# Two transformer-like layers on one NeuronCore: the value products of attention uncut, and for two key tiles in one visit; constant activation biases

## What is computed

```python
x = _layernorm(x + _L0_attn_ref(x, ...))              # RWKV time mix and channel mix
x = _layernorm(x + _L0_xattn_ref(x, ctx_1024, mask))  # cross attention, 16 heads of 16, masked
x = _layernorm(x + _L0_ffn_ref(x, ...))               # SwiGLU with int weights
x = _layernorm(x + _L1_attn_ref(x, ...))              # RMS norm, RG-LRU, gated MLP
x = _layernorm(x + _L1_xattn_ref(ctx_1024, x, ...))   # queries: x, keys: context, 16 heads of 16
x = _layernorm(x + _L1_ffn_ref(x, ...))               # 8 experts, top 2
```

## Time and profile before

| | |
|---|---|
| median of 3 runs | 2336.97 us (2332.34 to 2337.36) |
| the profiled execution, its own time | 2334.47 us |
| its span | 2332.6 us |
| TensorE busy | 1915.1 us (82%), 9728 instructions |
| VectorE busy | 1112.3 us (48%) |
| ScalarE busy | 967.2 us (41%) |
| GpSimd busy | 221.6 us (9%) |
| value products L1056 | 4352 instructions of 256 columns, 349.1 us busy |
| score products L1080 | 1088, 370.9 us busy |
| first-pass products L1014 | 1280, 356.3 us busy |
| score exponentials L1162 | 1088, 593.8 us busy, idle before them 332.7 us |
| maxima L1207 | 512, 496.6 us busy, idle before them 129.0 us |

### The profile page before, as it was taken

The page is one execution under the profiler, slowest core; times in us unless marked ns, Lnnn a source line. Parts: engine busy times, 40 slices in busy tenths (PEclk is TensorE's granted clock), DMA queues, the critical chain, the costliest instruction groups (busy, mean ns, idle before and its releaser), DMA issues.

```text
span 2332.6 us, 31610 instructions
## 1 busy us (share of the span) xinstructions
PE 1915.1 (82%) x9728; PEld 819.8 (35%) x9729; DVE 1112.3 (48%) x1498; ACT 967.2 (41%) x1638; POOL 221.6 (9%) x188
## 2 busy tenths in 40 slices
PE   5789869999798757727999999999999539999980
PEld 2334323333343222312333333333332326666650
DVE  3652358774212415418877777767760401121115
ACT  2422317667211443310477677667677102222220
POOL 2030100000200103200000000000000240000005
PEclk8889979999899888965999999999999669999995
DMA  7000051011000000092000000000000720000003
GB/s 270 0 0 0 9 124 28 23 27 58 1 0 0 4 0 30 9 133 76 1 15 9 10 13 8 10 14 9 8 2 1 320 72 27 27 27 27 27 25 108
DMA packets 63288, 90.59 MB, mean 39 GB/s; under 512 B 14144, under 2 KB 56320, under 8 KB 61514
## 3 DMA queue, kind: packets, MB, share of 16 engines
q1 hardware_dynamic: 60106, 80.77, 12.0%
q0 software_dynamic: 3072, 8.39, 1.1%
HBM read 61.53 MB, written 27.20 MB: 38 GB/s over the span
## 4 chain that ended last, share of the span: by engine, by line
PE 55%; DVE 6%; issue 4%; POOL 3%; ACT 2%; DMA 2%; SPq 1%; DVEq 0%; ACTq 0%; POOLq 0%
PE ps L1056 9%; PE ps L1014 8%; PE ps L1699 8%; PE ps L512 8%; PE ps L1080 8%; PE ps L1714 5%; DVE arena L1207 2%; PE ps L1357 2%; DMA qparts<-arena 1%; POOL rows_in L1808 1%; PE ps L1115 1%; POOL arena L1813 1%; PE ps L440 1%; PE ps L1707 1%; ACT arena L1767 1%
## 5 line engine op out<-in xcount | busy, mean ns | idle before, releaser
L1162 ACT ACTIVATE arena<-ps 128x512 f32<-128x512 f32 x1088 | 593.8, 598 | 332.7 <-PE ps L1080 331.9
L1207 DVE TENSOR_REDUCE arena<-ps 128x1 f32<-128x802 f32 (+1 forms) x512 | 496.6, 990 | 129.0 <-PE ps L1014 119.9
L512 PE MATMUL ps<-arena 128*128 x832 | 380.6, 618 | 83.9 <-DVE arena L1498 24.5
L1014 PE MATMUL ps<-arena 97*128 97x401 bf16 (+2 forms) x1280 | 356.3, 362 | 80.0 <-DMA arena<-qparts 62.2
L1080 PE MATMUL ps<-arena 100*128 100x512 bf16 x1088 | 370.9, 383 | 9.2 <-issue 8.5
L1056 PE MATMUL ps<-arena 128*32 128x256 f32 x4352 | 349.1, 393 | 0.7 <-ACT arena L1162 0.3
L512 PEld LDWEIGHTS ps<-arena 128*128 128x128 f32 x832 | 163.1, 198 | 299.5 <-issue 299.5
L1699 PE MATMUL ps<-arena 128*128 x608 | 199.1, 470 | 29.2 <-ACT arena L1767 28.4
L1014 PEld LDWEIGHTS ps<-arena 97*128 97x128 bf16 x1280 | 94.7, 99 | 293.8 <-issue 167.2
L1894 DVE TENSOR_TENSOR arena<-ps,arena 128x352 f32<-128x352 f32 x76 | 39.9, 525 | 273.0 <-ACT arena L1774 273.0
L1204 DVE TENSOR_REDUCE arena<-ps 128x2 f32<-128x1024 f32 x128 | 154.3, 1220 | 25.6 <-PE ps L1014 25.6
(11 more groups left out here) (183 smaller groups left out, 1409.9 us busy)
## 6 DMA issues: line engine op xcount, KB each, us to landing
arena<-in_experts_w SPq DMA_DIRECT2D x8, 2176.0 KB, 17.7
arena<-qparts SPq DMA_DIRECT2D x192, 64.0 KB, 2.3
qparts<-arena SPq DMA_DIRECT2D x24, 256.0 KB, 6.0
rows_in<-arena SPq DMA_DIRECT2D x1, 5120.0 KB, 32.7
arena<-kparts SPq DMA_DIRECT2D x12, 416.0 KB, 23.9
arena<-rows_in SPq DMA_DIRECT2D x38, 128.0 KB
rows_out<-arena SPq DMA_DIRECT2D x38, 128.0 KB, 1.7
arena<-in_w_rwkv SPq DMA_DIRECT2D x1, 2560.0 KB, 12.5
```

Source lines behind the costliest of these rows:

```text
L512: ins = eng.matmul(out, w[:, k, m * P:(m + 1) * P], x[:, k, tok(c)], start=k == 0, stop=k == ktiles - 1)
L1014: ins = eng.matmul(slot_banks(s_static)[:, x, 0:n_keys], Qst[0:97, ring, heads[x], q * P:(q + 1) * P], Kst[0:97, ring * HG + heads[x], at: ...
L1162: eng.activation(probs[:, keys_of(u, kt) % 2, h, :], ring_bank(r), ACT.Exp, bias=0.0).then_inc(ring_read.sem, 1)
L1207: eng.tensor_reduce(MX[:, par, heads[0] * QT + q, n % 2:n % 2 + 1], got, AX.XY, ALU.max).then_inc(slot_free.sem, 1)
```

## The change

The value products are no longer cut: one product of 512 queries for each head and tile. In the second attention (not in the window) they are sent out for two tiles in one visit, at tiles 2, 4, 6, 8 and 10, behind score 2; tile 0 of the next unit sends out the last three. `probs` gets two more buffers there (`more_probs`, in the field `WB`, whose weights are no longer needed). The copy of bank 4 stays behind the fourth exponential of tile 0. The five bias columns, their memsets and the wait for them go; every activation gets its constant as a number. The fields of `arena` behind them move by 20 bytes.

```diff
+UNSCALE = 0.5 * float(np.log(RMS_SCALE))
...
-        eps_col = f32(area(1), 1)
-        wkv_eps_col = f32(area(1), 1)
-        one_col = f32(area(1), 1)
-        zero_col = f32(area(1), 1)
-        unscale_col = f32(area(1), 1)
...
         probs = f32(a0, 2, HG, CH)
+        more_probs = f32(WB, 2, HG, CH)
...
-            for col, value in ((eps_col, LN_EPS), (wkv_eps_col, WKV_EPS), (one_col, 1.0), (zero_col, 0.0),
-                               (unscale_col, 0.5 * float(np.log(RMS_SCALE)))):
-                eng.memset(col, value).then_inc(cols_set, 1)
...
-            eng.wait_ge(cols_set, 5)
...
                 with eng.Fori(0, NC) as c:
                     eng.activation(norm_rstd[:, tok(c)], norm_rstd[:, tok(c)], ACT.Exp,
-                                   bias=zero_col if centre else unscale_col, scale=-0.5).then_inc(rstd.sem, 1)
+                                   bias=0.0 if centre else UNSCALE, scale=-0.5).then_inc(rstd.sem, 1)
...
-            PV_CUTS = 2
-            PVW = CH // PV_CUTS
+            TOGETHER, PROBS = (1, 2) if window or a == 0 else (2, 4)
...
+            def values_groups(kt, u):
+
+                last = (n_kt - TOGETHER) // TOGETHER * TOGETHER
+                if kt == 0:
+                    return [(t, -1) for t in range(last, n_kt)] if u > 0 else []
+                return [(t, 0) for t in range(kt - TOGETHER, kt)] if kt % TOGETHER == 0 and kt <= last else []
+
             def plan(u):
...
                     yield ("scores", kt, 2)
-                    if has_values:
-                        yield ("pv",) + values + (0,)
+                    for tile, before in values_groups(kt, u):
+                        yield ("pv", tile, before)
                     if mine[1] is not None:
                         yield ("item", mine[1])
                     yield ("scores", kt, 3)
-                    if has_values:
-                        yield ("pv",) + values + (1,)
...
+            def probs_of(n):
+                return (more_probs if n % PROBS >= 2 else probs)[:, n % 2, :, :]
...
-                def values(w, kt, cut):
-                    at = cut * PVW
+                def values(w, kt):
                     for h in range(HG):
-                        ins = eng.matmul(o_bank[32 * h:32 * h + 32, at:at + PVW], Vaug[:, kt, (w % 4) * HG + h, :],
-                                         probs[:, keys_of(w, kt) % 2, h, at:at + PVW],
-                                         start=kt == 0 and cut == 0, stop=kt == n_kt - 1 and cut == PV_CUTS - 1,
+                        ins = eng.matmul(o_bank[32 * h:32 * h + 32, :], Vaug[:, kt, (w % 4) * HG + h, :],
+                                         probs_of(keys_of(w, kt))[:, h, :], start=kt == 0, stop=kt == n_kt - 1,
                                          skip_group_check=True)
-                    if cut == PV_CUTS - 1:
-                        ins.then_inc(pv_done.sem, 1)
+                    ins.then_inc(pv_done.sem, 1)
...
-                            if h == 0 and (u > 0 or kt >= 2):
-                                pv_done.wait(eng, n_kt * i + kt - 1)
-                            eng.activation(probs[:, keys_of(u, kt) % 2, h, :], ring_bank(r), ACT.Exp,
+                            if h == 0 and (u > 0 or kt >= PROBS):
+                                pv_done.wait(eng, n_kt * i + kt - (PROBS - 1))
+                            eng.activation(probs_of(keys_of(u, kt))[:, h, :], ring_bank(r), ACT.Exp,
                                            bias=0.0).then_inc(ring_read.sem, 1)
...
+                            if step == ("scores", 0, HG - 1) and u > 0:
+                                copy_o(u, i)
...
-                        elif step == ("pv", n_kt - 1, -1, PV_CUTS - 1):
-                            copy_o(u, i)
```

More of the change, by code:

```diff
@@ L545, in _ @@
                 mix.wait(eng, c, 2)
[L546 removed]
+                eng.activation(B2[:, :, tok(c)], ps[:, 2:4, :], ACT.Exp, bias=0.0).then_inc(w_exp.sem, 1)
                 k_sub.wait(eng, c)
[L548 removed]
+                eng.activation(B3[:, :, tok(c)], B3[:, :, tok(c)], ACT.Exp, bias=0.0).then_inc(k_exp.sem, 1)
             eng.preload_act_table_set(SIGMOID)
@@ L551, in _ @@
                 r_out.wait(eng, c)
-                eng.activation(B1[:, :, tok(c)], B1[:, :, tok(c)], ACT.Sigmoid, bias=zero_col).then_inc(r_sig.sem, 1)
+                eng.activation(B1[:, :, tok(c)], B1[:, :, tok(c)], ACT.Sigmoid, bias=0.0).then_inc(r_sig.sem, 1)
             eng.preload_act_table_set(LN_EXP)
@@ L660, in _ @@
                     key.wait(eng, c, j + 1)
-                    eng.activation(keys[:, j, :], ps[:, j % 4, :], ACT.Relu, bias=zero_col).then_inc(relu.sem, 1)
+                    eng.activation(keys[:, j, :], ps[:, j % 4, :], ACT.Relu, bias=0.0).then_inc(relu.sem, 1)
                 rec.wait(eng, c)
-                eng.activation(B4[:, :, tok(c)], ps[:, 4:6, :], ACT.Sigmoid, bias=zero_col).then_inc(c_sig.sem, 1)
+                eng.activation(B4[:, :, tok(c)], ps[:, 4:6, :], ACT.Sigmoid, bias=0.0).then_inc(c_sig.sem, 1)
         @part("pool")
@@ L886, in plan @@
                     taken = max(taken, want)
-                    values = (kt - 1, 0) if kt else (n_kt - 1, -1)
-                    has_values = kt > 0 or u > 0
                     yield ("scores", kt, 0)
@@ L1082, in unit @@
                         elif what == "pv":
-                            _, kt, before, cut = step
+                            _, kt, before = step
                             if before:
@@ L1087, in unit @@
                                 ring_read.wait(eng, ring_before(i) + (ring_place(u, ("scores", kt, HG - 1)) + 1))
-                            if kt == 0 and cut == 0 and u > 0:
+                            if kt == 0 and u > 0:
                                 o_copied.wait(eng, i)
-                            values(u + before, kt, cut)
+                            values(u + before, kt)
                         elif what == "item":
@@ L1121, in _ @@
                 ring_read.wait(eng, ring_before(16))
-                for cut in range(PV_CUTS):
-                    values(7, n_kt - 1, cut)
+                for tile, _ in values_groups(0, 8):
+                    values(7, tile)
                 denominators(8, 16, 0)
@@ L1367, in _ @@
                     h_done.wait(eng, c, max(j - 1, 0))
-                    eng.activation(ffn_s[:, j % 2, :], ps[:, 2 * (j % 2), :], ACT.Silu, bias=zero_col,
+                    eng.activation(ffn_s[:, j % 2, :], ps[:, 2 * (j % 2), :], ACT.Silu, bias=0.0,
                                    scale=DEQUANT).then_inc(silued.sem, 1)
@@ L1455, in _ @@
                 lin.wait(eng, c)
-                eng.activation(B2[:, :, tok(c)], B1[:, :, tok(c)], ACT.Gelu, bias=zero_col).then_inc(lin_gelu.sem, 1)
+                eng.activation(B2[:, :, tok(c)], B1[:, :, tok(c)], ACT.Gelu, bias=0.0).then_inc(lin_gelu.sem, 1)
             eng.preload_act_table_set(SIGMOID)
@@ L1470, in _ @@
                 for h in range(2):
-                    eng.activation(B4[:, h, tok(c)], B4[:, h, tok(c)], ACT.Exp, bias=zero_col,
+                    eng.activation(B4[:, h, tok(c)], B4[:, h, tok(c)], ACT.Exp, bias=0.0,
                                    scale=rate[:, h:h + 1]).then_inc(a_exp.sem, 1)
@@ L1474, in _ @@
                 a_exp.wait(eng, c)
-                eng.activation(XC[:, :, tok(c)], B4[:, :, tok(c)], ACT.Square, bias=zero_col).then_inc(a_sq.sem, 1)
+                eng.activation(XC[:, :, tok(c)], B4[:, :, tok(c)], ACT.Square, bias=0.0).then_inc(a_sq.sem, 1)
             eng.preload_act_table_set(SQRT)
@@ L1478, in _ @@
             with eng.Fori(0, NC) as c:
-                eng.activation(XC[:, :, tok(c)], XC[:, :, tok(c)], ACT.Sqrt, bias=one_col,
+                eng.activation(XC[:, :, tok(c)], XC[:, :, tok(c)], ACT.Sqrt, bias=1.0,
                                scale=-1.0).then_inc(a_root.sem, 1)
@@ L1556, in _ @@
                 m_sig.wait(eng, c)
-                eng.activation(B1[:, :, tok(c)], B1[:, :, tok(c)], ACT.Gelu, bias=zero_col).then_inc(m_gelu.sem, 1)
+                eng.activation(B1[:, :, tok(c)], B1[:, :, tok(c)], ACT.Gelu, bias=0.0).then_inc(m_gelu.sem, 1)
         @part("dve")
@@ L1760, in _ @@
             eng.wait_ge(chain, CHAIN_EXP)
-            eng.activation(wts[:, 1, :], wts[:, 0, :], ACT.Exp, bias=zero_col).then_inc(r_exp, 1)
+            eng.activation(wts[:, 1, :], wts[:, 0, :], ACT.Exp, bias=0.0).then_inc(r_exp, 1)
             def copy_rows(j, u):
@@ L1773, in silu_half @@
                     eng.wait_ge(e_h, j * 2 + (half - 1))
-                eng.activation(silu[:, half, :], ps[:, 2 * half, 0:HALF], ACT.Silu, bias=zero_col).then_inc(e_silu, 1)
+                eng.activation(silu[:, half, :], ps[:, 2 * half, 0:HALF], ACT.Silu, bias=0.0).then_inc(e_silu, 1)
             def copy_hidden(j):
```

20 lines of the change are left out of this document (9 added, 11 removed).

## The result

The changed kernel took 2379.74 us (median of four runs, 2373.90 to 2382.78) against 2334.65 before: ratio 1.0191, 95% interval 1.0164 to 1.0218. The forecast was slower, 2357, range 2330 to 2376: right in sign, less than half the size. The profiled execution took 2373.9, span 2372.1, which is 39.5 over the span before; it was the fastest of its four.

A forecast was written before the change was run, and what follows sets the result against it. It took TensorE as the bound before (59.70 of 60 us busy) and the two slots after. Terms 17.8 + 11.6 - 4.6 - 5 = +20 took the profiled 2334.5 to 2354.5; median forecast 2357 us, range 2330 to 2376.

The forecast's parts named there:

- Pair of key tiles, 6.18: Second attention, two key tiles with items: 6.18 us from value block to value block, against 6.15 before.
- turn pair 7.36: Second attention, pair followed by the turn of the maxima, which waits for the last reduction: 7.36 against 6.63, +0.73.
- Units with items, +17.8 for 14 units: Second attention: pairs, turn and three-tile block lengthen units with items, less savings at the output products; +17.8 us.
- sign of 88% busy: Sign of being right: TensorE's busy share about 88% in second-attention pairs with items.
- Pair without items, 5.22: Units 6 and 7 of the second attention: a pair takes 5.22 us against 4.44, ScalarE idling about 1.2.
- Clock: the step that failed: The summed terms let TensorE keep its full clock; a drop to half was only a rival, 5%.
- Window, -4.6: First attention, window of 4 tiles: losing the cut saves 4.6 us in all.
- Biases, -5: Constant biases save 0.08 us on each of 60 activations on the path: -5 us.
- Arena shift, 0: Arena fields moving by 20 bytes: 0, between -3 and +3 us.
- A: Rival: TensorE stays the bound everywhere, so its shorter work makes the kernel faster, 2243 us; 8%.
- B: Rival: near even, shorter block or waits resolving sooner; 2339 us, between 2328 and 2345; 20%.
- C: Rival: TensorE drops to half clock in units 6 and 7, pairs 7.0 us, +23, total 2380; 5%.

The follow-up runs named there:

- experiment 10: The changed kernel itself, run again unaltered to look at its clock: 2376.47 us, ratio 1.0179 to the kernel before.
- experiment 4: Changed kernel with the second key tile's values one item and one score behind the first's, in two blocks: 2349.36 us, ratio 1.0073 to the kernel before.
- experiment 6: Changed kernel, still two tiles together, one item moved ahead of the value block in second-attention tiles with items: 2343.49 us, ratio 1.0048.
- experiment 8: Against experiment 7: order SSSIVSI or SISSSIVI, turn waiting only for its own slot, values in halves in units without items: 2303.89 us, ratio 0.9873.
- experiment 2: Kernel before with constant biases and values uncut in the window attention only: 2330.82 us, ratio 0.9987.
- experiment 11: Changed kernel, one key tile at a time, item ahead of values in both attentions, turn's own-slot wait, halves in units without items: 2287.02 us, ratio 0.9802.
- experiment 1: Kernel before with every bias column replaced by its constant, nothing else: 2331.43 us, ratio 0.9986.
- experiment 7: Order of experiment 6, but one key tile's values at a time, uncut, with two probability buffers: 2302.97 us, ratio 0.9875.
- experiment 5: Changed kernel with the second attention's turn of the maxima waiting only for the slot it writes (the turn's own wait): 2362.05 us, ratio 1.0133.

## Why the prediction was right, and where it was wrong

- **Pair of key tiles, 6.18; turn pair 7.36.** Measured 6.18 and 7.35. Right, with the block at 1.86 to the next item (1412.03 to 1413.88) and 1.92 long.
- **Units with items, +17.8 for 14 units.** Measured without the clock: 12 x 1.41 = 17, some 0.7 in the first unit (49.46 in experiment 10 against 48.75), and one unit's share in the first of the last three intervals. Right. Experiments 4 and 6 show that its reason, that the slots bind in TensorE's place, is the cause. Its sign of 88% busy was wrong: TensorE is busy 5.87 of the 6.18 in a pair (1425.56 to 1431.74). The prediction's sum goes from start to start (0.22 for a score), busy time counts each product to its end (0.38).
- **Pair without items, 5.22.** Measured 5.21. Right; but the three last intervals, for which the prediction's terms give 2.3 + 5.3 + 5.3 = 12.9 (the first with one plain unit's 1.3), grew by 3.0, 7.8 and 7.0. With the turn's own wait they grew by 1.7, 5.5 and 6.7, and of the 6.7 the last block takes 1.4, 4.14 at the half clock instead of 2.78. So the terms for the last two hold, and what is above them in the changed kernel is clock.
- **Clock: the step that failed.** The sum was made as if TensorE kept its full clock, and the clock stood among the rivals at 5%, for units 6 and 7 only. It fell instead behind single waits that the change makes or lengthens: the turn's 1.06 to 1.15 (0.30 before), the passages into and between the units without items, the 1.08 ahead of the last block. From its first score on, the second attention took 43.5 more, where the terms gave 29.4. Of the 14.1 missing, clock is some 10: 1.6 in the first unit, 3.3 in two plain units, 4.9 in the last three intervals (17.8 less 12.9). Another 3.0 stand in the passages of the loop, which the prediction put at nothing; about 2.0 of it is the longer wait at the two jumps. The last 1.3 are the units' own terms, each a little short. That wait is 3.3 to 3.9 in every kernel that takes two tiles together and 2.1 to 3.2 in the others, except experiment 8 with 3.2 and 3.7; why, no run shows. Removing the turn's wait saves 12 to 18 us in the timed runs, of which the steady unit explains 5. The page of the Trainium skill "TensorE: Matmul & The Clock Gate", section A second HAM failure mode, named by the prediction for this rival, speaks of frequent short idles between groups of products. The trace agrees only so far that short waits go ahead of the half clock: the single waits of 1.06 stand in an engine otherwise busy. The pairs without items, with some 0.26 of waiting for ScalarE before the fourth score, ran at 1.00 from 1778 to 1790; at 0.83 the row from 1790 to 1800 has a longer wait, 0.68 at 1795.
- **Window, -4.6.** Measured -2.5 in the trace, -2.0 in experiment 2. The mis-sized term is the 0.43 saved per unit: 0.22 was. The prediction let the slots bind in the second attention and left them out in the window; experiment 11, where the order alone brings 0.65 per unit, shows that they bind there too.
- **Biases, -5.** -3.3 (-1.2 to -5.4). The step's size holds (555 to 466 ns for the experts' Silu; the 710 of the earlier trace rows became 618 in experiment 1), so its count of 60 activations on the path was somewhat high.
- **Arena shift, 0.** Not tested by itself; experiment 1 has it too, inside its -3.3.
- **The rivals.** A (TensorE stays the bound, 2243) named its condition rightly: items issued ahead of the block. Experiment 7 meets it, by the order and one tile at a time, and there TensorE is busy 59.87 of 60 again. B did not come. C came in part: single blocks at half clock, most of them outside units 6 and 7, not whole pairs.

By sum: the prediction's +19.8 against the measured +39.5 is short by 14.1 in the second attention from its first score on, by 2.1 in the window and by 3.4 outside the attentions, where the change was to bring -5 and this one execution shows -1.6 (-0.3, +1.4 and -2.7).

What stays open: what exactly makes the clock fall. The turn's wait goes ahead of the half clock in all seven slowed units of the two profiles of the changed kernel, but it isn't enough by itself. Most turns there have the wait and no half clock behind it, and experiments 4 and 6 have it too (TensorE's idle before 14 turns sums to 15.1 and 14.5, against 15.1 in the changed kernel) and show no slowed unit in their one profile each.

## What to carry to other kernels

A long block on one engine is paid for by what lies ready for the others when it starts. Before making a block longer, count how much work the buffers between the engines hold, and put the consumer's next input ahead of the block, not behind it; here that order is worth 1.6 us of 42.6 per unit, and, with one key tile at a time, it turned a change that lost 45 us into kernels that win 29 to 46. Where the buffers can't cover the block (the units without items, three banks for 1 us), keep it cut.

## What the runs showed of the hardware

- The half clock costs in fixed portions, 1.62 per unit struck, but which units are struck differs between two executions of one program (the first three, then four others). Between profiles of different kernels a stretch of identical code ahead of the second attention took anything from 536.9 to 543.4.
- Removing a wait can bring more than the steady unit shows: 0.32 per unit, 5 us over 15 turns, but 12 to 18 us in all; in the profile its plain units keep the full clock. It can also bring less than its length: of the turn's 1.06 only 0.32 came off the steady unit, because the next wait was for the same maximum.
- The turn takes one of the two slots, so an item issued close behind it waits for the maximum of the last item ahead of it: 0.40 in experiment 5, 0.76 in experiment 8.
